# Cross-attention and MoE layer on one core: the four attention projections as three f16 products with split weights and split inputs instead of one f32 product

## What is computed

```python
q = (x @ Wq).reshape(b, n, N_HEADS, HEAD_DIM)          # x: normed, 128 x 256 per batch
k, v = jnp.split(ctx @ Wkv, 2, axis=-1)                # ctx: 128 x 128 per batch
q = apply_axial_rope(q, pos_map)
k = apply_axial_rope(k, ctx_pos_map)
logits = jnp.einsum('bqhd,bkhd->bhqk', q, k) * scale
w = jax.nn.softmax(logits, axis=-1)
attn = jnp.einsum('bhqk,bkhd->bqhd', w, v)
return attn.reshape(b, n, N_HEADS * HEAD_DIM) @ Wout + bout
...
x = x + _L0_xattn_ref(_layernorm(x), ctx_1024, ...)
x = x + _L0_ffn_ref(_layernorm(x), ...)
```

## Time and profile before

| | us |
|---|---|
| median of 3 executions | 429.85 |
| lowest and highest | 429.79, 432.39 |
| profiled execution | 428.33 |
| its span, first to last instruction | 426.6 |
| mean granted TensorE clock in the profiled execution, share of full speed | 0.911 |

### The profile page before, as it was taken

The page is one execution under the profiler, slowest core; times in us unless marked ns, Lnnn a source line. Parts: engine busy times, 40 slices in busy tenths (PEclk is TensorE's granted clock), DMA queues, the critical chain, the costliest instruction groups (busy, mean ns, idle before and its releaser), DMA issues. The chain is left out here.

```text
span 426.6 us, 9168 instructions
## 1 busy us (share of the span) xinstructions
PE 317.8 (74%) x2986; PEld 212.4 (50%) x2986; DVE 236.8 (55%) x624; ACT 201.3 (47%) x378; POOL 167.3 (39%) x241
## 2 busy tenths in 40 slices
PE   0473878999999999999986588797988996775000
PEld 0251646777777777777664234454566543331000
DVE  6464447677777777777774457999682321221000
ACT  2232456776777777776774663535724121110000
POOL 9342144233344444443000200443785225776720
PEclk9997689999999999999999589999999999996555
DMA  7898276211111111103200235110336694222255
GB/s 191 252 256 238 55 211 193 55 35 31 31 32 32 31 32 25 31 23 91 62 18 2 75 125 206 25 51 1 101 102 206 198 245 109 28 26 26 28 94 111
DMA packets 35035, 39.27 MB, mean 92 GB/s; under 512 B 8032, under 2 KB 29120, under 8 KB 34752
## 3 DMA queue, kind: packets, MB, share of 16 engines
q1 hardware_dynamic: 24082, 21.55, 17.6%
q10 hardware_dynamic: 8030, 11.93, 9.7%
q0 software_dynamic: 2896, 5.44, 7.4%
HBM read 26.36 MB, written 10.32 MB: 86 GB/s over the span
## 5 line engine op out<-in xcount | busy, mean ns | idle before, releaser
L476 DVE TENSOR_REDUCE mx<-bank 128x4 f16<-128x512 f32 x128 | 87.2, 684 | 30.0 <-PE bank L576 29.9
L369 ACT ACTIVATE pw<-bank 128x512 f32<-128x512 f32 x128 | 76.8, 601 | 52.0 <-PE bank L600 31.0
L247 POOL TENSOR_TENSOR rot<-t 128x256 f32<-128x256 f32 x30 | 21.1, 726 | 108.1 <-DVE t L469 108.1
L576 PE MATMUL bank<-kz,qst 128*128 128x512 f16 x128 | 51.1, 400 | 7.2 <-DMA kz<-kT 5.9
L589 PE MATMUL bank<-qst,kz 128*128 128x128 f16 x512 | 50.7, 223 | 6.5 <-DMA qst<-mxs 5.9
L589 PEld LDWEIGHTS bank<-qst,kz 128*128 128x128 f16 x512 | 38.3, 100 | 19.4 <-issue 7.5
L600 PE MATMUL bank<-pw,V 128*32 128x128 f32 x1024 | 34.7, 276 | 0.0
L877 POOL DMA_INDIRECT out<-ac,dst x16 | 21.7, 1354 | 28.6 <-DVE ac L1118 10.4
L1118 DVE TENSOR_SCALAR ac<-mbank,wpair 128x256 f32<-128x256 f32 x16 | 7.7, 484 | 44.0 <-DMA odd<-ac,dst 41.2
L1175 PE MATMUL mbank<-hT,WSG 128*128 128x512 f16 (+1 forms) x144 | 32.0, 379 | 0.0
L600 PEld LDWEIGHTS bank<-pw,V 128*32 128x32 f32 x1024 | 25.9, 109 | 8.8 <-issue 7.5
(11 more groups left out here) (175 smaller groups left out, 645.9 us busy)
## 6 DMA issues: line engine op xcount, KB each, us to landing
ring_gu<-in_L_ffn_w_gate_up ACTq DMA_DIRECT2D x20, 352.0 KB
kz<-kT SPq DMA_DIRECT2D x64, 64.0 KB, 2.0
ring_dn<-in_L_ffn_w_down ACTq DMA_DIRECT2D x10, 352.0 KB
ring_gu<-in_L_ffn_w_gate_up SPq DMA_DIRECT2D x8, 352.0 KB
X<-in_x SPq DMA_DIRECT2D x4, 512.0 KB, 7.4
...
```

The lines of the kernel that those rows point to most:

```text
L247: eng.tensor_tensor(rot[:, part], t1[:, part], t2[:, part], ALU.add).then_inc(rot_ok[w], 1)
L369: act.activation(pw[g % 4][:, :], STB[g % 2][:, :], ACT.Exp, scale=SCALE).then_inc(exp_ok, 1)
L476: dve.tensor_reduce(mx[u // 2 % 2][:, u % 2:8:2], SB[u % 2][:, :].rearrange("p (j t) -> p j t", j=4), axis=AX.X, op=ALU.max, negate=True). ...
L576: pe.matmul(SB[u % 2][:, :], qst[m.par][:, u, :], kz[m.par][:, :, u, :], start=True, stop=True).then_inc(s_mm, 1)
```

## The change

Each weight matrix is loaded as f32 into memory that is otherwise used later (WKV and WQ into raw_wsg, WO into the tile OT), and is split once: ACT writes the f16 rounding of 64 times the weight (the tuple `halves`, three activations, behind the norm of batch 0), and DVE writes the f16 rest (three SCALAR_TENSOR_TENSOR, each behind its activation). PE begins only when all three rests are there (`w_lo` 3). In each period the copies of xcT and attnT out of PSUM by ACT now write the f16 rounding, and DVE subtracts it from the PSUM tile and writes the f16 rest: `rest_xcT` at the end of step g = 0 and `rest_attnT` at the end of step g = 5. Only behind these do the projections start. Each f32 product becomes three f16 products (high x high, high x low, low x high) that sum up in PSUM. The factor 64 is taken out again where the result is read: in the rotation tables, in the copy of V, and in the sum into X. The memory of the weights keeps its size, since two f16 parts take what one f32 takes.

```diff
--- before.py
+++ after.py
@@ -37,6 +37,7 @@
 QUADS, SLOT = NH // 4, 32
 DK = D // P
 MAXROW = 3 * HD
+THREE = (0, 0), (0, 1), (1, 0)
 HALF = SLOT // 2
 SCALE = float(1.0 / np.sqrt(np.float32(HD)))
 EPS = 1e-5
@@ -162,14 +163,14 @@
 
 
         POS = sb("POS", [P, NB, 2])
-        WQ = sb("WQ", [P, DK, D])
-        WKV = sb("WKV", [P, 2 * D])
-        WO = sb("WO", [P, DK, D])
+        WQ = sb("WQ", [P, 2, DK, D], F16)
+        WKV = sb("WKV", [P, 2, 2 * D], F16)
+        WO = sb("WO", [P, 2, DK, D], F16)
         BO = sb("BO", [P, D])
         identh = sb("identh", [P, P], F16)
         CT = [sb(f"CT{i}", [P, DC]) for i in range(2)]
         xn = sb("xn", [P, D])
-        xcT = [sb(f"xcT{i}", [P, 3, P]) for i in range(2)]
+        xcT = [sb(f"xcT{i}", [P, 2, 3, P], F16) for i in range(2)]
         t1 = sb("t1", [P, 2 * D])
         t2 = sb("t2", [P, 2 * D])
         rot = sb("rot", [P, 2 * D])
@@ -185,7 +186,7 @@
         OT = sb("OT", [P, 4, P])
         rec = sb("rec", [P, NH // 2, 2])
         attn = sb("attn", [P, D])
-        attnT = sb("attnT", [P, DK, P])
+        attnT = sb("attnT", [P, 2, DK, P], F16)
         st1 = sb("st1", [P, NB, 6])
         mv1 = sb("mv1", [P, NB, 2])
         rs1 = sb("rs1", [P, NB, 1])
@@ -193,6 +194,11 @@
         ang = sb("ang", [P, 2, NB, 2, 2])
         turns = sb("turns", [P, 2, NB, 2, 2])
         raw_wsg = sb("raw_wsg", [P, DK, 2 * SHARED])
+        raw_qkv = raw_wsg[:, :, :].rearrange("p c f -> p (c f)")
+        raw_wq, raw_wkv = raw_qkv[:, 0:2 * D], raw_qkv[:, 2 * D:4 * D]
+        raw_wo = OT[:, :, :].rearrange("p q t -> p (q t)")
+        halves = [(raw_wkv, WKV[:, 0, :], WKV[:, 1, :])] + [
+            (raw, w[:, 0].rearrange("p c n -> p (c n)"), w[:, 1].rearrange("p c n -> p (c n)")) for raw, w in ((raw_wq, WQ), (raw_wo, WO))]
         RC = sb("RC", [P, NB, 4, 2])
         RS = sb("RS", [P, NB, 4, 2])
 
@@ -209,6 +215,7 @@
         turn_s, sin_s, rope_tab = sem("turn_s"), sem("sin_s"), sem("rope_tab")
         xn_ok, x_biased = sem("xn_ok"), sem("x_biased")
         xcT_mm, xcT_ok = sem("xcT_mm"), sem("xcT_ok")
+        w_hi, w_lo, xcT_hi, attnT_hi = sem("w_hi"), sem("w_lo"), sem("xcT_hi"), sem("attnT_hi")
         qk_mm, rope_ok, tokst_ok = sem("qk_mm"), sem("rope_ok"), sem("tokst_ok")
         rot_ok, hi_ok = ([sem(f"{n}_{w}") for w in "qk"] for n in ("rot_ok", "hi_ok"))
         qstT_mm, kstT_mm, qst_ok, kT_ok = sem("qstT_mm"), sem("kstT_mm"), sem("qst_ok"), sem("kT_ok")
@@ -269,9 +276,9 @@
                 sp.dma_start(X[:, 4 * c:4 * c + 4, :], xr[:, 4 * c:4 * c + 4, :]).then_inc(x_in[c], 16)
                 if c == 0:
                     sp.dma_start(CT[0][:, :], ctx_in[0]).then_inc(ctx_in_s[0], 16)
-                    sp.dma_start(WQ[:, :, :], wq.rearrange("(c p) n -> p c n", p=P)).then_inc(w_in, 16)
-                    sp.dma_start(WKV[:, :], wkv).then_inc(w_in, 16)
-                    sp.dma_start(WO[:, :, :], wout.rearrange("(c p) n -> p c n", p=P)).then_inc(w_in, 16)
+                    sp.dma_start(raw_wkv, wkv).then_inc(w_in, 16)
+                    sp.dma_start(raw_wq.rearrange("p (c n) -> p c n", c=DK), wq.rearrange("(c p) n -> p c n", p=P)).then_inc(w_in, 16)
+                    sp.dma_start(raw_wo.rearrange("p (c n) -> p c n", c=DK), wout.rearrange("(c p) n -> p c n", p=P)).then_inc(w_in, 16)
                     sp.dma_start(BO[:, :], bout.rearrange("(a n) -> a n", a=1).broadcast_to([P, D])).then_inc(bo_in, 16)
 
             def period(b):
@@ -356,9 +363,12 @@
             def evac_xcT(m):
                 at_least(act, xcT_mm, m.n + 1)
                 at_least(act, v_mm, m.n - 1)
-                act.copy(xcT[m.par][:, :, :], M1[:, 0:3 * P].rearrange("p (c t) -> p c t", c=3)).then_inc(xcT_ok, 1)
+                act.copy(xcT[m.par][:, 0], M1[:, 0:3 * P].rearrange("p (c t) -> p c t", c=3)).then_inc(xcT_hi, 1)
 
             norm(Batch(0, 0))
+            act.wait_ge(w_in, 48)
+            for raw, hi, lo in halves:
+                act.activation(hi, raw, ACT.Copy, scale=WUP).then_inc(w_hi, 1)
 
             def period(b):
                 m1, m2, m3, m4, o = b + 1, b + 2, b + 3, b + 4, b + -1
@@ -371,7 +381,7 @@
                         at_least(act, v_mm, m1.n + 1)
                         act.wait_ge(consts, 6)
                         at_least(act, pv_mm, QUADS * b.n)
-                        act.copy(Vh[m1.par][:, :, :, 0:HD], M0[:, 0:D].rearrange("p (f h d) -> p f h d", f=2, d=HD)).then_inc(v_ok, 1)
+                        act.activation(Vh[m1.par][:, :, :, 0:HD], M0[:, 0:D].rearrange("p (f h d) -> p f h d", f=2, d=HD), ACT.Copy, scale=1 / WUP).then_inc(v_ok, 1)
                     if g == 0 and inside(m3):
                         evac_xcT(m3)
                     if g == 1 and inside(m1):
@@ -394,7 +404,7 @@
                     if g == 5 and inside(o):
                         act.wait_ge(attnT_mm, o.n + 1)
                         at_least(act, wo_mm, o.n)
-                        act.copy(attnT[:, :, :], M0[:, D:2 * D].rearrange("p (c t) -> p c t", c=DK)).then_inc(attnT_ok, 1)
+                        act.copy(attnT[:, 0], M0[:, D:2 * D].rearrange("p (c t) -> p c t", c=DK)).then_inc(attnT_hi, 1)
                     if g == 6 and inside(m2):
                         at_least(act, kstT_mm, m2.n + 1)
                         if inside(m1):
@@ -402,6 +412,8 @@
                         act.copy(kT[:, :, :], M1[:, :].bitcast(F16).rearrange("p (q t) -> p q t", q=QUADS)).then_inc(kT_ok, 1)
 
             def evac_OT(m):
+                if isinstance(m.n, int) and m.n == 0:
+                    act.wait_ge(w_lo, 3)
                 act.wait_ge(pv_mm, QUADS * m.n + QUADS)
                 at_least(act, ob_mm, m.n)
                 act.copy(OT[:, :, :], OB[m.par][:, :].rearrange("p (q t) -> p q t", q=4)).then_inc(OT_ok, 1)
@@ -442,8 +454,8 @@
                     sin = ang[:, 0].rearrange("p b a f -> p b (a f)")
                     cos = ang[:, 1].rearrange("p b a f -> p b (a f)")
                     for r in range(2):
-                        dve.tensor_copy(RC[:, :, :, r], cos)
-                        dve.tensor_scalar(RS[:, :, :, r], sin, -1.0 if r == 0 else 1.0, None, ALU.mult).then_inc(rope_tab, 1)
+                        dve.tensor_scalar(RC[:, :, :, r], cos, 1 / WUP, None, ALU.mult)
+                        dve.tensor_scalar(RS[:, :, :, r], sin, (-1.0 if r == 0 else 1.0) / WUP, None, ALU.mult).then_inc(rope_tab, 1)
                 dve.wait_ge(std1, k + 1)
                 dve.reciprocal(rs1[:, a:e, 0], rs1[:, a:e, 0]).then_inc(rs1_ok, 1)
                 dve.wait_ge(rs1_ok, 2 * k + 1)
@@ -452,6 +464,19 @@
 
             statistics(0, 4, 0)
             dve.wait_ge(mx_zero, 2)
+            for n, (raw, hi, lo) in enumerate(halves):
+                dve.wait_ge(w_hi, n + 1)
+                dve.scalar_tensor_tensor(out=lo, in0=raw, scalar=WUP, in1=hi, op0=ALU.mult, op1=ALU.subtract).then_inc(w_lo, 1)
+
+            def rest_xcT(m):
+                at_least(dve, xcT_hi, m.n + 1)
+                dve.tensor_tensor(xcT[m.par][:, 1], M1[:, 0:3 * P].rearrange("p (c t) -> p c t", c=3), xcT[m.par][:, 0],
+                                  ALU.subtract).then_inc(xcT_ok, 1)
+
+            def rest_attnT(m):
+                dve.wait_ge(attnT_hi, m.n + 1)
+                dve.tensor_tensor(attnT[:, 1], M0[:, D:2 * D].rearrange("p (c t) -> p c t", c=DK), attnT[:, 0],
+                                  ALU.subtract).then_inc(attnT_ok, 1)
             dve.wait_ge(rope_tab, 3)
 
             def rope_cos(m):
@@ -498,7 +523,8 @@
                     if g == 7 and inside(o):
                         dve.wait_ge(wo_mm, o.n + 1)
                         dve.wait_ge(x_biased, o.n + 1)
-                        dve.tensor_tensor(X[:, o.n, :], M0[:, 0:D], X[:, o.n, :], ALU.add).then_inc(x1_ok, 1)
+                        dve.scalar_tensor_tensor(out=X[:, o.n, :], in0=M0[:, 0:D], scalar=1 / WUP, in1=X[:, o.n, :],
+                                                 op0=ALU.mult, op1=ALU.add).then_inc(x1_ok, 1)
                     if g == 3 and inside(m3):
                         rope_cos(m3)
                     if g % 2 == 1:
@@ -514,6 +540,10 @@
                         dve.bn_stats(st2[:, o.n, :], X[:, o.n, :]).then_inc(st2_ok, 1)
                     if g == 3 and inside(o):
                         normalise(o)
+                    if g == 0 and inside(m3):
+                        rest_xcT(m3)
+                    if g == 5 and inside(o):
+                        rest_attnT(o)
                     if g == 4 and inside(m3):
                         rope_sin(m3)
                     if g == 4 and isinstance(b.n, int) and b.n == -3:
@@ -540,11 +570,13 @@
 
             def project_k(m):
                 at_least(pe, xcT_ok, m.n + 1)
-                pe.matmul(M1[:, D:2 * D], xcT[m.par][:, DK, :], WKV[:, 0:D], start=True, stop=True)
+                for i, (a, w) in enumerate(THREE):
```

(17 more changed lines are left out.)

## The result

The changed kernel takes 434.3 us (median; 428.6 to 436.9), the kernel before 428.8 on the same chip (424.5 to 433.6). The ratio is 1.0098, 95% interval 1.0059 to 1.0136: slower by 4.2 us. The ratio and its interval leave out, for both kernels, the slow executions, which are those over 1.5% above the kernel's fastest, and so 434.3 over 428.8 comes to more (1.0128). The middle lies within 1%, the upper end of the interval beyond it. The profiled execution took 433.61 with a span of 431.9, against 428.33 and 426.6. A second measurement of both, unchanged, gave 1.0097.

What follows compares the result with a forecast made beforehand. The prediction took a ring of DVE, a transfer and PE to bound the loop, and transfers the start. Profiled 428.33 + 2.5 (start) + 0.4 (end) - 0.2 (loop) = 431.0; the median 1.5 above gives 432.5, range 427.0 to 438.0.

Steps and rivals of the forecast that it cites:

- my three classes: Whole time against no change: faster (below 425.5) 0.12, within one per cent 0.61, slower (above 434.2) 0.27.
- What bounds the kernel: Attention loop and start: the loop is bound by a cycle of DVE, transfer and PE, 11.49 us; the start by transfers.
- The ring of DVE, transfer and PE: Loop period: DVE work to the maxima's copy 3.72, their transfer 2.50, PE to project_q's end 5.27; 11.49 us in all.
- the third part: Loop period: PE from the maxima's landing to project_q's end, 5.27 us; only PE time here shortens the period directly.
- The products: Projections: three f16 products cost 0.33 us against 0.43 for one f32, saving 0.6 per period; at 0.215 each, a loss.
- The subtractions in the loop: Loop: xcT 0.56 us, attnT 0.42; project_k 0.28 late; stalls eat the saving, -0.2 over twelve periods, bounds -1.2 to +1.8.
- PE bound after all: Loop rival: halves come early or waits move into existing holes; each period shrinks 0.6 us, giving 425.3; chance 0.17.
- The maxima come late: Loop rival: maxima's copy queues behind the subtraction and delays later scores, 0.5 us a period, giving 438.5; chance 0.20.
- The start: Before the loop, to the end of the wait for the keys: split and subtractions add 2.5 us, bounds 0 and +3.2.
- The start is hidden: Start rival: transfers alone set the end of the keys' wait, so the 2.5 us goes, giving 430.0; chance 0.13.
- The end: Batches 13 to 15: nothing covers the subtraction before project_out; +0.4 us, bounds 0 and 0.8.

Runs made afterwards that it cites:

- e4_maxfirst: Changed kernel, but DVE copies the maxima of g = 1 ahead of the subtraction of xcT; ratio to the kernel before 1.0044.
- e7_lateload: Changed kernel, but the loads of WSD and gw that ACT issues in period 13 come one period later; ratio to the kernel before 1.0126.
- e8_klater: Changed kernel, but PE does project_k directly ahead of project_q, behind the score products of g = 2; ratio to the kernel before 1.0059.
- e5_start: Kernel before with only the split of the three weights added at the start, results unused, and PE's wait for them; ratio to the kernel before 1.0013.
- e2_dummy: Kernel before with f32 products, only the two subtractions and the waits for them added, results unused; ratio to the kernel before 1.021.
- e3_early: Changed kernel, but weights split ahead of batch 0's norm and PE waits for the rests only at its first projection; ratio to the kernel before 1.0018.

## Why the prediction was right or wrong

The forecast was 432.5 with a range of 427 to 438, and the likeliest of my three classes was "within 1%". The median came out at 434.3 with a ratio of 1.0098, within that class by its middle. The sum that I expected above the profiled kernel before was 2.7; by the ratio on one chip it is 4.2 (428.81 x 0.0098), with an interval of 2.5 to 5.8 that just holds the 2.7. The mechanism held. The term of the loop was low by 0.4; that of the end was low too, by an amount that the profiles leave open.

- **What bounds the kernel: held, one sentence too strong.** The ring of DVE, transfer and PE stands in the rows after with 3.73, 2.52 and 5.43. "PE work outside the third part is followed by a wait" fell with the subtractions on the f32 kernel: 0.62 a period instead of 0.3. PE's own work sets the pace as soon as it grows by some 0.3.
- **The products: right.** 0.11 apart, three cost 0.33, the f32 one 0.43. The other bound, 0.215 a product, did not appear. The estimate from the Trainium skill, page "TensorE: Matmul & The Clock Gate", section "Back-to-back issue gap", 0.24 to 0.39 for three, holds the 0.33, but the 0.11 of one is just half of the 0.22 of 512 columns.
- **The subtractions in the loop: right, and for the reason given.** 0.56 and 0.40 (forecast 0.56 and 0.42), `project_k` waiting 0.26 (forecast 0.28), periods 11.41 to 11.69 with a mean of 11.550; 11.533 less the forecast 0.02 is 11.51. The term was -0.2 for twelve periods; 12 x 0.017 makes it +0.2.
- **PE bound after all (425.3): false as put, but near.** It asked that the halves come early or that the waits move into existing holes. Without subtractions the period does fall, to 11.06, but by 0.47 and not by 0.6. `project_k` placed later does just this for one of the two waits, and gives 0.2 of the 0.5.
- **The maxima come late (438.5): false in the loop.** Their copy comes 0.5 later, as reckoned, and the period is the same with it moved back (11.549). A wait of this kind does appear, in period 13 alone, where I had not looked.
- **The start: the right place, and about the right size.** I took +2.5 with 3.2 as its upper bound; the first `logits_q` moved by 3.13 and 3.27 in two pairs, but by only 1.9 to 2.1 in e4_maxfirst, e7_lateload and e8_klater, whose start is the same. The mean of the five is 39.35, 2.5 behind the mean of before (36.90). That it hits the forecast so well is luck: the point scatters by 1.3. What repeats is the issue of the keys' transfer, at 30.8 against 27.9 and 27.5. Its parts, against 27.93: the split alone +2.4 (e5_start, 30.37), the subtractions alone +1.65 (e2_dummy, 29.58), both with the f16 products +2.9; so the shorter products give some 1.2 back, where I had put 0.6 for batch 0 alone. The first PE row was 2.49 late and not 2.1 to 2.2: each activation took the 0.61 reckoned but they started 0.52 apart, while DVE's three took 0.80, 0.68 and 0.68, and PE started 0.10 behind the last. The 3.27 that batch 2 waits behind DVE's statistics was missed in the forecast; here the keys' transfer covers it. With the split moved early the ratio falls from 1.0098 to 1.0018: by this the start is the larger part of the loss, though the split alone (e5_start) shows 0.13% only.
- **"The start is hidden" (430.0): false for its reason.** DMA share 0.87 instead of 0.99: the queue did start later. How much of the 2.7 of the split is returned afterwards is open, since that kernel alone is not told from before by its times.
- **The end: low.** I reckoned +0.4 for three waits of `project_out`. From the last `project_q` of the loop to the mixture was 44.9 and 43.8 before, 46.7 and 44.7 after, so +0.9 to +1.8 by pairs; e3_early and e4_maxfirst, with the same end, have 48.9 and 46.5. The waits of L656 grew as reckoned (0.46 at batch 14). Divided at the last transpose of maxima for which PE waits (before at 225.00 and 222.44, after at 228.07 and 226.64), the last part is 12.60 and 11.65 before, 12.61 and 11.97 after, so at most 0.3 more for two of the three waits. What is longer lies ahead of that point: 32.3 and 32.1 before, 34.1 and 32.8 after. The wait for the maxima in period 13 (1.36 and 0.57) is most of that, and its cause stays open.

So the answer to where the gain went: the exchange saves 0.5 us of PE in each period; the weights of these products are now the output of a subtraction that PE must wait for, and that wait is as long as the saving. What is left is the price of the split and of the subtractions at the start, and something at the end.

A cure that was not tried is to start the two products with the high part before the subtraction is done. `project_k` writes into the bank that the subtraction reads, and over part of its columns. The Trainium skill, page "PSUM — Partial Sum Buffer", section "PSUM bank collisions raise a hardware error", says that no two engines may touch one bank in the same partitions at a time, whichever columns; no run here shows it. The order would need another bank for the output, and this kernel uses all eight.
